# Cross-attention on one core: the first four pairs' folds of a group placed inside the last unit of the group before

## The reference, cut to what matters

```python
# x (16, 1024, 512), context (16, 64, 512), 16 heads of 64; mask (16, 1024, 64), Wq/Wk/Wv (512, 1024), Wo (1024, 512)
qh = (x @ Wq + bq).reshape(16, 1024, 16, 64)
kh = (context @ Wk + bk).reshape(16, 64, 16, 64)
vh = (context @ Wv + bv).reshape(16, 64, 16, 64)
attn = einsum('bqhd,bkhd->hbqk', qh, kh) * mask
attn = attn - max(attn)                      # one maximum over everything
attn = exp(attn) * mask
attn = attn / (sum(attn, axis=-1) + 1e-15)
out = einsum('hbqk,bkhd->bqhd', attn, vh).reshape(16, 1024, 1024) @ Wo + bo
y = layernorm(out + x) * gamma + beta
```

## Time and profile before

| | before |
|---|---|
| median of 3 runs | 1663.99 us (1663.68 to 1664.08) |
| the profiled execution's own time | 1665.72 us |
| its span, first to last instruction | 1663.9 us |
| busy: PE, DVE, ACT, POOL | 97%, 67%, 53%, 27% |
| mean granted TensorE clock | 0.994 of full speed |

### The profile page before, as it was taken

One profiled execution on the slowest core, in us unless ns is written; L12 is line 12 of the kernel. 1 busy time (PEld: TensorE's weight loads), 2 busy tenths in 40 slices (PEclk: granted clock), 3 DMA queues, 4 the chain that ended last, 5 costly groups with the idle time before them and its releaser, 6 DMA issues. The chain is left out here.

```text
span 1663.9 us, 32320 instructions
## 1 busy us (share of the span) xinstructions
PE 1618.6 (97%) x11804; PEld 791.4 (48%) x11804; DVE 1122.5 (67%) x2253; ACT 885.9 (53%) x1357; POOL 444.5 (27%) x768
## 2 busy tenths in 40 slices
PE   5999999999999999999999999999999999999998
PEld 4555455555554555555544444444444444444443
DVE  6656464655465645645464888878787877888785
ACT  5555454544444545445445665556655665566641
POOL 0000000000000000000000466556565566556655
PEclk9999999999999999999999999999999999999999
DMA  7383544542644537344435756665565556665412
GB/s 251 142 294 96 194 181 140 207 155 107 235 140 172 194 106 263 99 178 171 159 127 203 296 228 231 250 249 206 221 232 212 214 206 226 252 240 203 178 61 76
DMA packets 81668, 315.95 MB, mean 190 GB/s; under 512 B 5408, under 2 KB 9760, under 8 KB 71840
## 3 DMA queue, kind: packets, MB, share of 16 engines
q1 hardware_dynamic: 81568, 314.47, 51.7%
HBM read 184.43 MB, written 130.02 MB: 189 GB/s over the span
## 5 line engine op out<-in xcount | busy, mean ns | idle before, releaser
L91 PE MATMUL ps_s<-x_hi,g_hi 128*128 128x512 f16 x1024 | 390.5, 381 | 0.0
L92 PE MATMUL ps_s<-x_lo,g_hi 128*128 128x512 f16 x1024 | 389.9, 381 | 0.0
L100 PE MATMUL ps_o<-u,p_hi 128*128 128x512 f16 x1024 | 388.8, 380 | 1.0 <-DMA u<-u_halves 1.0
L93 PE MATMUL ps_s<-x_hi,g_lo 128*128 128x512 f16 x1024 | 389.5, 380 | 0.0
L101 PE MATMUL ps_o<-u,p_hi 128*128 128x512 f16 x1024 | 388.1, 379 | 0.0
L102 PE MATMUL ps_o<-u,p_lo 128*128 128x512 f16 x1024 | 388.1, 379 | 0.0
L535 ACT ACTIVATE s<-ps_s,c_bias 128x512 f32<-128x512 f32 x256 | 176.1, 688 | 363.8 <-PE ps_s L93 353.5
L663 DVE TENSOR_TENSOR score_max<-score_max,tile_max 128x1 f32<-128x1 f32 x257 | 40.5, 158 | 331.8 <-ACT s L535 331.2
L733 POOL PARTITION_ALL_REDUCE key_max<-early_max x1 | 0.7, 713 | 874.4 <-DVE early_max L672 874.4
L1313 POOL TENSOR_TENSOR y<-y,gamma_b 128x512 f32<-128x512 f32 x124 | 157.6, 1271 | 233.5 <-ACT y L1044 233.5
L1031 ACT ACTIVATE p_hi<-ps_bc 128x512 f16<-128x512 f32 x256 | 151.3, 594 | 86.7 <-DVE ps_bc L1179 86.5
(11 more groups left out here) (132 smaller groups left out, 2301.7 us busy)
## 6 DMA issues: line engine op xcount, KB each, us to landing
scores<-s SPq DMA_DIRECT2D x30, 2048.0 KB, 7.8
x<-xT_in SPq DMA_DIRECT2D x32, 1024.0 KB, 10.0
u_halves<-u_out SPq DMA_DIRECT2D x64, 512.0 KB, 3.0
u<-u_halves SPq DMA_DIRECT2D x16, 2048.0 KB, 7.9
s_more<-scores SPq DMA_DIRECT2D x16, 2048.0 KB, 7.8
y<-x_in SPq DMA_DIRECT2D x32, 1024.0 KB, 9.9
out<-y SPq DMA_DIRECT2D x31, 1024.0 KB, 4.3
s<-scores SPq DMA_DIRECT2D x14, 2048.0 KB, 7.9
```

What stands on the lines that cost most here:

```text
L91: pe.matmul(out, lhs_hi, rhs_hi, start=first, stop=False)
L92: pe.matmul(out, lhs_hi, rhs_lo, start=False, stop=False)
L93: return pe.matmul(out, lhs_lo, rhs_hi, start=False, stop=last)
L100: pe.matmul(out, lhs_hi, rhs_hi, start=False, stop=False, skip_group_check=True)
```

## The change

The folds of pairs 0 to 3 and the `bias` of every group but the first leave the start of their group. They stand now in unit 3 of the group before: folds 0 and 1 behind tile 3, folds 2 and 3 behind tile 5, then all 32 bias matmuls in one row. ACT's and DVE's parts of them move along. DVE's final copy into `c_bias` is made in two steps, one for each batch entry: the first behind the folds, the second at the start of the group, when ACT no longer reads the old values; `c_ready` counts two a group and ACT waits for it at units 0 and 2. In unit 3 the mask is made behind tile 0 and no longer behind tile 5 (in unit 1 it stays behind tile 5). Group 0 has no unit before it: its folds stay ahead, with the bias behind fold 1. The work itself is the same. No transfer is moved in SP's program.

```diff
+        early_folds = {3: (0, 1), 5: (2, 3)}
...
             def project_values(g, first):
-                pe.wait_ge(c_ready, g + 1)
+                pe.wait_ge(c_ready, 2 * g + 1)
...
-            def bias(g, pairs):
-                for p in pairs:
+            def bias(g):
+                for p in range(NP):
...
-                if p == NP - 1:
-                    mm.then_inc(c_summed, 1)
+                mm.then_inc(c_summed, 1)
...
-            def scores(g, u, first):
+            def scores(g, u, first, last):
...
                     if p in quad_behind[u]:
                         fold_o(g, quad_behind[u][p])
+                    if u == UNITS - 1 and not last and p in early_folds:
+                        for pair in early_folds[p]:
+                            fold_q(g + 1, pair, False)
+                        if p == max(early_folds):
+                            bias(g + 1)
 
             def group(g, first, last):
-                for p in range(EARLY):
-                    fold_q(g, p, first)
-                    bias(g, (2 * p, 2 * p + 1))
                 for u in range(UNITS):
...
             pe.wait_ge(bq_done, 2)
+            for p in range(EARLY):
+                fold_q(0, p, True)
+                if p == 1:
+                    bias(0)
             group(0, True, False)
...
             def round_g(g, p):
-                if p == 0:
-                    act.wait_ge(s_summed, (g * UNITS + 2) * NP)
+                if p == 0 and not (isinstance(g, int) and g == 0):
+
+                    act.wait_ge(s_summed, (g * UNITS + 1) * NP + EARLY)
...
-                if u == 0:
-                    act.wait_ge(c_ready, g + 1)
+                if u % UB == 0:
+                    act.wait_ge(c_ready, 2 * g + u // UB + 1)
...
+                    if u == UNITS - 1 and not last and p in early_folds:
+                        for pair in early_folds[p]:
+                            round_g(g + 1, pair)
                     if p == NP // 2 and not (last and u == UNITS - 1):
                         round_x(g, u + 1)
...
             def bias(g):
                 dve.wait_ge(c_summed, g + 1)
-                dve.wait_ge(s_out, g * UNITS * NP + SBANKS)
...
+                dve.wait_ge(c_added, 2 * g + 2)
+                bias_of(0)
+
+            def bias_of(b):
+
                 for h in range(2):
-                    dve.wait_ge(c_added, 2 * g + h + 1)
-                    for b in range(GB):
-                        of_keys = dve.tensor_scalar(c_bias[rows_of(h), :, b], c_sum[rows_of(b), h, :], 1.0, None, ALU.mult)
+                    of_keys = dve.tensor_scalar(c_bias[rows_of(h), :, b], c_sum[rows_of(b), h, :], 1.0, None, ALU.mult)
                 of_keys.then_inc(c_ready, 1)
...
+                    if u == UNITS - 1 and not last and p in early_folds:
+                        for pair in early_folds[p]:
+                            split_g(g + 1, pair)
+                        if p == max(early_folds):
+                            bias(g + 1)
                     if p == NP // 2 and not (last and u == UNITS - 1):
                         split_x(g, u + 1)
...
-                    if p == NP // 2 + 1 and u % UB == 1 and not (last and u == UNITS - 1):
+                    if p == (NP // 2 + 1 if u < UNITS - 1 else 0) and u % UB == 1 and not (last and u == UNITS - 1):
                         mask(g, (u + 1) // UB)
 
             def group(g, first, last):
-                for p in range(EARLY):
-                    split_g(g, p)
-                bias(g)
+
+                dve.wait_ge(s_out, g * UNITS * NP + SBANKS)
+                bias_of(1)
```

More of the change, by code:

```diff
@@ L429, in scores @@
                         fold_o(g, quad_behind[u][p])
+                    if u == UNITS - 1 and not last and p in early_folds:
[3 more added lines that the diff above has]
+                            bias(g + 1)
             def group(g, first, last):
-                for p in range(EARLY):
-                    fold_q(g, p, first)
-                    bias(g, (2 * p, 2 * p + 1))
                 for u in range(UNITS):
-                    scores(g, u, first)
+                    scores(g, u, first, last)
                     if u == 0:
@@ L563, in group @@
             def group(g, first, last):
-                for p in range(EARLY):
-                    round_g(g, p)
                 for u in range(UNITS):
@@ L576, in _ @@
             round_x(0, 0)
+            for p in range(EARLY):
+                round_g(0, p)
             group(0, True, False)
@@ L720, in _ @@
             mask(0, 0)
+            for p in range(EARLY):
+                split_g(0, p)
+                if p == 1:
+                    bias(0)
             group(0, True, False)
```

## The result

| | before | after |
|---|---|---|
| median of 4 runs each, taken together | 1663.84 us (1663.06 to 1664.08) | 1651.49 us (1651.09 to 1652.13) |
| the profiled execution's own time | 1665.72 us | 1651.50 us |
| its span | 1663.9 us | 1649.7 us |
| mean granted TensorE clock | 0.994 | 0.996 |

After to before is 0.9933, with a 95% interval of 0.992 to 0.9946; the two medians alone give 0.9926. The change is worth 12.35 us where 16.5 were forecast. The time is 4.0 us above the forecast of 1647.5 and 2.0 us above the upper end of the forecast's own range, 1645.5 to 1649.5. One of the timed runs, of experiment 3, took 2351.08 us at a mean granted clock of 0.675 and is in none of the medians and ratios here.

A forecast was written before the change was run, and what follows sets the result against it. PE, busy 1618.6 of 1663.9 us, was taken as the bound. Gains of 11.5 + 4.8 + 0.2 = 16.5 us off the profiled 1665.72 gave 1649.2, less 1.73 to the median: 1647.5 us, range 1645.5 to 1649.5.

The forecast's parts named there:

- What bounds the kernel now: PE bounds the kernel; at group starts four folds fill four banks and wait for DVE's late `g_lo`, 10.9 us together.
- Each of the seven starts gives back 1.64 us, together 11.5: At later group starts, a 5.16 us block goes and two insets plus bias, 3.52 us, replace it.
- Rival 2: The 32 bias matmuls in one row run slower, 0.91 instead of 0.44 us: 1650.8 us; chance 0.04.
- A fall costs 1.6 us, three cost 4.8: Clock drops to 1.2 GHz around three of seven group starts go with the stall; bounds 0 to 4.8 us.
- rival 1: Half-array folds and bias, not the stall, lower the clock; three falls stay: 1652.3 us; chance 0.09.
- I take the same distance off: The profiled execution stood 1.73 us above the median; the same was subtracted from 1649.2, giving 1647.5 us.
- Tile 7 followed by tile 0 after 0.22 us at every group start: Sign expected in the profile after: ordinary 0.22 us matmul spacing across each group start.
- Group 0: 0.2 us: Group 0's folds and 3.1 us stall stay; two bias bursts move ahead of the stall, saving 0.2 us, bounds 0 and 0.4.
- What was costed at nothing: Unit 3's moved work fits: `kv_lo` slips some 0.5 us with 1.9 spare; fold 2's banks have 2.3 us or more.
- rival 3: Fold 2 finds its banks 1 us late, so 7 us of the gain go: 1654.5 us; chance 0.05.
- rival 4: Keys (`kv_lo`) come late for the folds behind tile 3, making the kernel slower, 1669.2 us at 5 us slip; chance 0.03.
- the stall is: Condition for the full 4.8 us clock gain: the stall at group starts, not the folds' work, lowers the clock.

The follow-up runs named there:

- experiment 3: Changed kernel with PE's hardware loop over the first phase's six middle groups written out; 1649.63 us, ratio 0.992.
- experiment 9: The kernel of experiment 8 with PE's loop of the first phase written out as well; 1649.75 us, ratio 0.9917.
- experiment 2: Kernel before, with only unit 3's mask moved to behind tile 0; 1663.99 us, ratio 1.0001.
- experiment 1: Kernel before, with six unused 128x512 matmuls filling the longer stall at each group start but the first; 1661.76 us, ratio 0.9991.
- experiment 4: Changed kernel with the first mask on DVE made behind group 0's splits, not ahead of them; 1647.39 us, ratio 0.9904.
- experiment 10: Changed kernel again, without an edit, for more timed runs and a second profile; 1651.04 us, ratio 0.9926.
- experiment 6: Kernel before again, without an edit, for a second profile of its clock; 1664.21 us.
- Experiment 5: Changed kernel with its two insets of folds one tile earlier, behind tiles 2 and 4 of unit 3; 1657.46 us, ratio 0.9969.
- experiment 8: Changed kernel with only folds 0 and 1 moved, behind tile 5; folds 2, 3 and the bias back at the group start; 1657.14 us, ratio 0.9969.

## Why the forecast was right in kind and 4 us short

- **"What bounds the kernel now", and the stall's cause**: right. PE's waits for `g_lo` are gone and the second phase moved ahead by all that the first gave. Experiment 9 shows the cause, four banks for four folds in a row. Experiment 2 strikes the mask from the chain: without it the wait stays.
- **"Each of the seven starts gives back 1.64 us, together 11.5"**: measured 1.69 each, 11.7 together. The insets are 1.76 and 2.14 us (forecast 1.76 and 2.20). The bias was costed at 0.44 us and adds 0.38: 32 matmuls at about 12 ns each, (454.93 - 454.55) / 31. By the floor of about 25 ns between starts in the Trainium skill, page "TensorE: Matmul & The Clock Gate" (Part 1), it would be an estimated 0.8 us. The trace does not agree for the row as a whole. But it has two chains side by side: the 16 matmuls into `ps_k` (rows 0 to 63) start (454.93 - 454.55) / 15 = 25 ns apart, and so do the 16 into `ps_both` (rows 64 to 127). So the distance that the page gives is there within one half of the rows, and the prediction's 14 ns comes from counting both halves. Rival 2 is out.
- **"A fall costs 1.6 us, three cost 4.8"; that they go with the stall**: right for the profiled pair, and rival 1 is out, since nothing behind group 0 in the first phase is below 1.00 in either profile of the changed kernel. What was wrong is how many falls a typical run had, the next point.
- **"I take the same distance off", 1.73 us, after "three cost 4.8 us"**: this is the step that failed; the branches and group 0, below, are the rest of the miss. The two terms were both taken, but the distance between the profiled execution and the median held part of the falls already. By the forecast's own prices the profiled execution without its falls would take 1665.72 - 4.8 = 1660.9 us; the lowest of 23 runs of before beside experiments 1 to 4 was 1660.68, their median 1663.41. After the change there was no such distance: 1651.50 profiled and 1651.49 in the median. Nor is it a constant of profiling: in experiment 2 it is +2.1 us, in experiment 10 -1.8.

  The mean granted clock that each timed run has on record bears this out, for it counts the falls without placing them. A window with a fall has 0.86 over 12 us, that is 3.4 us at half speed, and 3.4 / 2 of 1664 us lowers the mean of a run by 0.001. The profiled execution had 0.994. The 45 timed runs of before beside the experiments average 0.9954; the six at 0.994 average 1664.6 us, the seven at 0.997 average 1661.6. Nine runs of the changed kernel (the result's and experiment 10's) average 0.9962. So an average run gained about 0.8 of such a stretch (group 0's included), an estimated 1.3 us and not 4.8. 11.7 (the groups) + 1.3 - 1.0 (the branches) = 12.0 us, where the medians differ by 12.35.
- **"Tile 7 followed by tile 0 after 0.22 us at every group start"**: true at the entry, in the last group and at one branch back of five. The others cost 1.0 us together. Before, folds stood behind the branch, with a stall after them that hid a late instruction: the two profiles of before have one such gap each, of 0.14 and 0.08 us, and the period around it is at most 0.05 us longer. The prediction named cover for every moved step but not for what the stall itself covered.
- **"Group 0: 0.2 us"**: the term holds, and group 0 still came out 1.2 us worse. The block from its first fold to tile 0 takes 8.72 us in both profiles of the changed kernel and 8.92 in experiment 1, where group 0's code is that of before, all with one long stretch at the low clock: 0.2 us better. The rest is that the folds began 0.64 us later (24.84 against 24.20 us), behind work that was not edited, and that the low clock held longer. Experiments 1 and 6 have the same 0.74 with the old code, and fold 4 starts at 35.21 us in experiment 10, 2.0 us earlier than in the other profile of the same kernel. It is one execution's state, and no range for it stood in the sum.
- **"What was costed at nothing"**: held. `kv_lo` slipped by 0.5 us, as forecast (it begins 7.42 us behind the unit's first matmul, before 6.95), and kept 1.8 us of spare (forecast 1.9); fold 2's banks had 2.6 us (forecast 2.3 or more); DVE's bias ended in time. Rivals 3 and 4 are out. Experiment 5 shows that rival 4's spare is real: one tile earlier it is gone.

Sum of the miss, by the profiled pair: 1.7 (the distance) + 1.4 (group 0, 1.2 in place of -0.2) + 1.0 (branches) - 0.2 (the groups) = 3.9 of 4.0 us.

What lowers the clock at a start is not settled. In the profiles, falls behind group 0 came only where four folds with bias stand together and a stall of 1.3 us lies among them (before, experiments 2 and 6), and there at three, three and one of seven starts. None was seen with the stall filled (experiment 1) or with the folds taken apart, and none behind stalls of 0.9 to 1.2 us beside two folds (5) or pauses of up to 1.65 us behind two folds (8). So neither the stall alone nor the folds alone were seen with a fall; the prediction's "the stall is" says more than that. But most of these kernels have a single profile, and with the old order too a start without a fall is more frequent than one with it. The mean clocks of the timed runs point the same way: 0.9954 before and 0.9950 in experiment 2, against 0.9960 to 0.9966 in experiments 1, 3, 5, 8, 9 and 10.

## What to carry to other kernels

Where a profiled execution is slower than the median, ask which of its losses the median lacks before you take off both the loss and the distance; the mean granted clock of every timed run can tell. When a stall is removed, list not only what hides the new work but what the stall hid: here late instructions behind a branch back, up to 0.4 us with long matmuls and up to 1.65 us with short ones. Two folds at a time fit the four banks without a wait for them, in the middle of a unit and at a group's start alike (experiment 9). The same kind of stall in group 0, twice as long and left as given, was worth 4.1 us more for one moved line (experiment 4).

## What the runs showed of the hardware

- PE's instructions come late behind a hardware loop's branch back: up to 0.4 us between tiles of 512 columns (in some passes nothing), 0.72 to 1.65 us in a row of two-column matmuls (experiment 8). They are not late where the loop is entered, nor at all when it is written out (experiments 3 and 9). The time lost is more than the idle column says: 0.38 us where it has 0.22, 7.4 us of median (7.1 of span) in five starts where it has 5.8.
- The granted clock is not the same from one execution of a program to the next. With the old order of folds there were three falls behind group 0 in two profiles (before, and experiment 2) and one in a third (experiment 6).
- Two-column matmuls start 25 ns apart within one half of the rows, and the two halves run side by side: 12 ns for one when both are counted (changed kernel, 454.55 to 454.93 us).
